# Attention: row maxima turned in squares of 32 by ScalarE and VectorE, not by TensorE, and a quarter of one block's sum moved from GpSimd to VectorE

## What is computed

```python
q = (x @ wq_w + wq_b).reshape(bs, sl, 32, 32)
k = (x @ wk_w + wk_b).reshape(bs, sl, 8, 32)
v = (x @ wv_w + wv_b).reshape(bs, sl, 8, 32)
attn = jnp.einsum('bqhfd,bkhd->bhfqk', qg, k) * scale     # qg: q with 4 heads for each key head
att = jax.nn.softmax(attn, axis=-1)
a = jnp.einsum('bhfqk,bkhd->bqhfd', att, v)
```

## Time and profile before

| | us |
|---|---|
| median of three timed runs | 2800.37 (2800.07 to 2800.58) |
| the profiled execution | 2795.91 |
| its span | 2794.1 |

### The profile page before, as it was taken

The page is one execution under the profiler, slowest core; times in us unless marked ns, Lnnn a source line. Parts: engine busy times, 40 slices in busy tenths (PEclk is TensorE's granted clock), DMA queues, the critical chain, the costliest instruction groups (busy, mean ns, idle before and its releaser), DMA issues.

```text
span 2794.1 us, 48987 instructions
## 1 busy us (share of the span) xinstructions
PE 2752.4 (99%) x14654; PEld 1695.8 (61%) x14654; DVE 2181.9 (78%) x2809; ACT 1529.4 (55%) x2959; POOL 1909.4 (68%) x710
## 2 busy tenths in 40 slices
PE   7999999999999999999999999999999999999998
PEld 4788888884444444444444444444444447888887
DVE  4433434348999999999999999999999968676667
ACT  3211111116777676777767777767777764455454
POOL 2433333317999999999999999999999996111110
PEclk9999999999999999999999999999999999999999
DMA  7544443434444334334334334344444443323332
GB/s 268 181 144 137 147 139 132 137 116 137 91 88 100 87 87 100 85 87 100 85 87 100 85 89 98 89 90 93 93 90 91 97 123 114 113 96 108 113 100 81
DMA packets 167645, 307.05 MB, mean 110 GB/s; under 512 B 50001, under 2 KB 91409, under 8 KB 159505
## 3 DMA queue, kind: packets, MB, share of 16 engines
q1 hardware_dynamic: 158496, 240.05, 29.5%
q0 software_dynamic: 9072, 66.06, 11.6%
HBM read 159.12 MB, written 79.82 MB: 86 GB/s over the span
## 4 chain that ended last, share of the span: by engine, by line
PE 74%; DVE 2%; ACT 0%; issue 0%; DVEq 0%; POOL 0%; ACTq 0%; POOLq 0%
PE back_ps L1348 22%; PE back_ps L1362 18%; PE s_ps L1322 17%; PE s_ps L1938 11%; PE back_ps L1379 2%; PE back_ps L1987 2%; PE back_ps L2006 1%; PE back_ps L1959 1%; DVE mx L1237 1%; PE back_ps L1337 0%; PE s_ps L1411 0%; DVE a_lo L1281 0%; ACT h_t L1719 0%; DVE two_sum L1252 0%; DVE xn L1793 0%
## 5 line engine op out<-in xcount | busy, mean ns | idle before, releaser
L1218 ACT ACTIVATE p_t<-back_ps 128x512 f32<-128x512 f32 x2048 | 1114.7, 596 | 432.5 <-PE back_ps L1348 390.7
L1237 DVE TENSOR_REDUCE mx<-s_ps 128x1 f32<-128x1024 f32 x1002 | 1172.4, 1208 | 83.9 <-PE s_ps L1322 76.2
L1128 POOL TENSOR_TENSOR p_sum<-p_sum,p_t 128x2048 f32<-128x2048 f32 x254 | 1166.2, 4591 | 24.8 <-ACT p_t L1218 7.9
L1348 PE MATMUL back_ps<-q_st,k_st 98*128 98x512 f32 x2048 | 809.9, 436 | 3.4 <-POOL ones L1097 2.4
L1348 PEld LDWEIGHTS back_ps<-q_st,k_st 98*128 98x128 f32 x2048 | 343.9, 187 | 592.1 <-ACT p_t L1218 495.7
L1322 PE MATMUL s_ps<-k_st,q_st 96*128 96x512 f32 x2004 | 633.0, 397 | 0.6 <-DVE mx L1237 0.3
L1362 PE MATMUL back_ps<-p_t,v_sb 128*32 128x512 f32 x4096 | 545.8, 605 | 0.0
L1322 PEld LDWEIGHTS s_ps<-k_st,q_st 96*128 96x128 f32 x2004 | 379.0, 189 | 72.5 <-DVE mx L1237 3.2
L574 POOL TENSOR_TENSOR o_lo<-side,o_hi 128x512 fp32r<-128x512 f32 x80 | 104.2, 1303 | 321.4 <-ACT o_hi L544 321.2
L1252 DVE TENSOR_REDUCE two_sum<-p_t 128x512 f32<-128x1024 f32 x256 | 317.8, 1243 | 2.1 <-ACT p_t L1218 2.1
L1128 POOL TENSOR_TENSOR p_sum<-p_t 128x2048 f32<-128x2048 f32 x64 | 312.9, 4889 | 8.6 <-ACT p_t L1218 8.6
(11 more groups left out here) (186 smaller groups left out, 2910.8 us busy)
## 6 DMA issues: line engine op xcount, KB each, us to landing
p_sum<-two_sum POOLq DMA_DIRECT2D x63, 1024.0 KB, 6.9
q_st<-q_hi_d SPq DMA_DIRECT2D x128, 256.0 KB, 4.3
stage<-w_mod SPq DMA_DIRECT2D x48, 512.0 KB, 6.4
q_hi_d<-o_hi SPq DMA_DIRECT2D x64, 256.0 KB, 2.0
q_lo_d<-o_lo SPq DMA_DIRECT2D x64, 256.0 KB, 2.0
q_st<-q_lo_d SPq DMA_DIRECT2D x64, 256.0 KB, 4.1
att_d<-a_sb SPq DMA_DIRECT2D x128, 128.0 KB, 2.3
a_f<-att_d SPq DMA_DIRECT2D x32, 512.0 KB, 4.6
```

The costliest lines, as they stand in the source:

```text
L1128: nc.gpsimd.tensor_tensor(total, before, p_t[:, kt, :, :], ALU.add).then_inc(sum_done, 1)
L1218: nc.scalar.activation(p_t[:, s, c, :], st_ps[:, c % 2, :], ACT.Exp, scale=SCALE)\
L1237: nc.vector.tensor_reduce(mx[:, slot % 2, e:e + 1], s_ps[:, e % 2, :], AX_X, ALU.max)\
L1348: nc.tensor.matmul(st_ps[:, c % 2, :], k_st[:, slot // 2, s * P:(s + 1) * P], q_st[:, slot, jj, h * QW:(h + 1) * QW], start=True, stop=True)\
```

## The change

The turn of the maxima leaves TensorE. ScalarE waits for the 16 maxima of a pair and rounds `mx` (128x16) to its high part, into the first 16 columns of a 128x32 tile `m_parts`, then writes the negated high part back beside the maxima. VectorE adds the two (a reduce of 16 pairs, so the low part) into the other 16 columns, waits for that, and turns the 128x32 tile in four squares of 32 into `m_rows`. A square holds 16 rows of high and 16 of low parts of 32 queries, so SP stores them by four DMAs of 32 rows of 128 bytes each, where there were two. The rows of `k_st` hold -1 instead of 1. The tiles are doubled by pair. The waits that shared the corner of `den_ps` with the turn go or are replaced.

Apart from this, in all pairs but the last, GpSimd adds only the columns 0 to 2 of block 2 (three quarters), and VectorE's fourth sum adds blocks 2, 3 and 4 of column 3 instead of 3 and 4. ScalarE's write of block 2 of the next pair therefore waits for VectorE's sums too.

```diff
+def put_rows(sp, q_st, slot, m_rows, landed):
+    rows = q_st[96:98, slot, :, :].bitcast(F32).rearrange("h j (t b r) -> h b (j t) r", b=4, r=32)
+    for b in range(4):
+        sp.dma_start(rows[:, b, :, :], m_rows[32 * b:32 * b + 32, slot % 2, :]).then_inc(landed, 16)
...
-    TURN_STEP = 5
+    MAX_STEP = 5
+    SHARED = 2
+    POOL_COLS = 3
...
         def put_max(pair, slot):
-            sp.wait_ge(m_lo_done, pair + 1)
-            for n, part in enumerate((m_hi, m_lo)):
-                sp.dma_start(q_st[STACK + n:STACK + n + 1, slot, :, :].bitcast(F32)
-                             .rearrange("o j s -> o (j s)"), part[:, :].bitcast(F32))\
-                  .then_inc(m_in, 16)
+            sp.wait_ge(m_turned, pair + 1)
+            put_rows(sp, q_st, slot, m_rows, m_in)
...
-                nc.gpsimd.tensor_tensor(total, before, p_t[:, kt, :, :], ALU.add).then_inc(sum_done, 1)
+                cols = slice(0, POOL_COLS if kt == SHARED and shares(pair) else REP)
+                nc.gpsimd.tensor_tensor(total[:, cols, :], before[:, cols, :], p_t[:, kt, cols, :], ALU.add)\
+                  .then_inc(sum_done, 1)
...
-        def max_hi(pair):
-            act.wait_ge(m_turned, pair + 1)
-            if not is_int(pair, 0):
-                act.wait_ge(m_in, pair * 32)
-            nc.scalar.activation(m_hi[:, :], m_ps, ACT.Copy, scale=-1.0).then_inc(m_hi_done, 1)
+        def max_hi(pair, slot):
+            act.wait_ge(max_done, pair * NS + NS)
+            if not below(pair, 2):
+                act.wait_ge(m_turned, pair - 1)
+            nc.scalar.copy(m_parts[:, slot % 2, 0:NS], mx[:, slot % 2, 0, :]).then_inc(m_hi_done, 1)
+            act.wait_ge(m_hi_done, pair + 1)
+            nc.scalar.activation(mx[:, slot % 2, 1, :], m_parts[:, slot % 2, 0:NS].bitcast(F32), ACT.Copy, scale=-1.0)\
+              .then_inc(m_back_done, 1)
...
-                    if c == 1 and s == TURN_STEP and not is_int(pair, NPAIR - 1):
-                        max_hi(pair + 1)
+                    if c == 1 and s == MAX_STEP and not is_int(pair, NPAIR - 1):
+                        max_hi(pair + 1, 1 - par)
...
-        def max_lo(pair):
-            dve.wait_ge(m_hi_done, pair + 1)
-            if not is_int(pair, 0):
-                dve.wait_ge(m_in, pair * 32)
-            nc.vector.scalar_tensor_tensor(m_lo[:, :], m_ps, -1.0, m_hi[:, :].bitcast(F32), ALU.mult,
-                                           ALU.subtract).then_inc(m_lo_done, 1)
+        def max_lo(pair, slot):
+            dve.wait_ge(m_back_done, pair + 1)
+            nc.vector.tensor_reduce(m_parts[:, slot % 2, NS:2 * NS].bitcast(F32),
+                                    mx[:, slot % 2, :, :].rearrange("p s e -> p e s"), AX_X, ALU.add)\
+              .then_inc(m_lo_done, 1)
+        def turn_max(pair, slot):
+            dve.wait_ge(m_lo_done, pair + 1)
+            if not below(pair, 2):
+                dve.wait_ge(m_in, pair * 64 - 64)
+            nc.vector.transpose(m_rows[:, slot % 2, :], m_parts[:, slot % 2, :].bitcast(F32)).then_inc(m_turned, 1)
...
-            nc.vector.tensor_reduce(two_sum[:, c, :], p_t[:, TWO:TWO + 2, c, :].rearrange("p s q -> p q s"),
+            first = SHARED if c >= POOL_COLS and shares(pair) else TWO
+            nc.vector.tensor_reduce(two_sum[:, c, :], p_t[:, first:TWO + 2, c, :].rearrange("p s q -> p q s"),
...
-                if s == TURN_STEP + 1 and not is_int(pair, NPAIR - 1):
-                    max_lo(pair + 1)
+                if s == MAX_STEP + 1 and not is_int(pair, NPAIR - 1):
+                    max_lo(pair + 1, slot + 1)
+                    turn_max(pair + 1, slot + 1)
...
-        def turn_max(pair, slot):
-            pe.wait_ge(max_done, pair * NS + NS)
-            if is_int(pair, 1):
-                pe.wait_ge(m_lo_done, 1)
-            elif not below(pair, 3):
-                pe.wait_ge(den_taken, pair - 2)
-            nc.tensor.matmul(m_ps, mx[:, slot % 2, :], ident[:, :], start=True, stop=True)\
-              .then_inc(m_turned, 1)
...
-                pe.wait_ge(m_in, pair * 32 + 32)
+                pe.wait_ge(m_in, pair * 64 + 64)
...
                 if s == SUM_STEP and not below(pair, 1):
-                    add_sum(pair - 1, (slot - 1) % 2)
-                if s == TURN_STEP and not is_int(pair, NPAIR - 1):
                     piece = piece_at(pair, slot % 2, it)
                     if piece:
                         pe.wait_ge(wo_lo_done, piece[1])
-                    turn_max(pair + 1, (slot + 1) % QR)
+                    add_sum(pair - 1, (slot - 1) % 2)
```

More of the change, by code:

```diff
@@ L124, in adaln_block @@
         m_at = k_at + 2 * S * 4 + 4 * 512 * 4
-        m_hi = keep("m_hi", [16, P], F32R)
-        m_lo = keep("m_lo", [16, P], F32R)
+        m_parts = keep("m_parts", [P, 2, 32], F32R)
+        m_rows = keep("m_rows", [P, 2, 32], F32)
+        mx = keep("mx", [P, 2, 2, 16], F32)
+        keep("m_rest", [P, 2 * P - 192], F32)
         assert nc.sbuf_base == m_at + 2 * P * 4
-        mx = keep("mx", [P, 2, 16], F32)
         s_ps = whole.enter_context(nc.psum_tensor("s_ps", [P, 2, S], F32))
-        ahead = Ahead(q_st, k_st, mx, m_hi, m_lo, s_ps, [sem(f"q_in{u}") for u in range(4)],
-                      [sem(f"k_in{u}") for u in range(2)], sem("s_ready"), sem("max_done"), sem("m_turned"),
-                      sem("m_hi_done"), sem("m_lo_done"), sem("m_in"),
+        ahead = Ahead(q_st, k_st, mx, m_parts, m_rows, s_ps, [sem(f"q_in{u}") for u in range(4)],
+                      [sem(f"k_in{u}") for u in range(2)], sem("s_ready"), sem("max_done"),
+                      sem("m_hi_done"), sem("m_back_done"), sem("m_lo_done"), sem("m_turned"), sem("m_in"),
                       [sem(f"qk_out{s}") for s in range(2)], [sem(f"v_out{s}") for s in range(2)])
@@ L473, in do @@
                         elif ev[0] == "negate":
-                            sp.wait_ge(ahead.m_lo_done, 1)
-                            for n, part in enumerate((ahead.m_hi, ahead.m_lo)):
-                                sp.dma_start(ahead.q_st[3 * HD + n:3 * HD + n + 1, 0, :, :].bitcast(F32)
-                                             .rearrange("o j s -> o (j s)"), part[:, :].bitcast(F32))\
-                                  .then_inc(ahead.m_in, 16)
+                            sp.wait_ge(ahead.m_turned, 1)
+                            put_rows(sp, ahead.q_st, 0, ahead.m_rows, ahead.m_in)
                         elif ev[0] == "rows":
@@ L781, in do @@
                             last.then_inc(ahead.s_ready, 1)
-                        elif ev[0] == "negate":
-                            pe.wait_ge(ahead.max_done, AHEAD - 3)
-                            nc.tensor.matmul(ahead.s_ps[0:16, 0, 0:P], ahead.mx[:, 0, :], ident[:, :],
-                                             start=True, stop=True).then_inc(ahead.m_turned, 1)
                         elif ev[0] == "group" and is_int(i, 0) and ev[1] < OBANKS:
@@ L895, in piece_at, with shares @@
         return two, (1 if is_int(pair, 1) else two + 2)
+    def shares(pair):
+        return not is_int(pair, NPAIR - 1)
     def below(i, value):
@@ L914, in sem @@
         return ctx.enter_context(nc.semaphore(name))
-    q_st, k_st, mx, m_hi, m_lo, s_ps = ahead.q_st, ahead.k_st, ahead.mx, ahead.m_hi, ahead.m_lo, ahead.s_ps
+    q_st, k_st, mx, s_ps = ahead.q_st, ahead.k_st, ahead.mx, ahead.s_ps
+    m_parts, m_rows = ahead.m_parts, ahead.m_rows
     p_t = sb("p_t", [P, NKT, REP, QW], F32)
@@ L1164, in await_bank @@
         def await_bank(pair):
-            if below(pair, 2):
-                act.wait_ge(m_lo_done, pair + 1)
-            else:
+            if not below(pair, 2):
                 act.wait_ge(den_taken, pair - 1)
@@ L1373, in add_sum @@
                 pe.wait_ge(joined, pair * 16 + 16)
-                if is_int(pair, NPAIR - 2):
-                    pe.wait_ge(den_taken, NPAIR - 2)
-                else:
-                    pe.wait_ge(m_lo_done, pair + 3)
+                if not below(pair, 1):
+                    pe.wait_ge(den_taken, pair)
             for c in range(REP):
```

43 lines of the change are left out of this document (23 added, 20 removed).

## The result

The changed kernel takes 2840.49 us (median of four runs, 2836.57 to 2844.15) against 2800.22 before: a ratio of 1.0145, interval 1.0132 to 1.0157. It is slower by 40 us. The profiled execution took 2844.15 us, with a span of 2842.3.

What follows compares the result with a forecast made beforehand. TensorE bounds the kernel at 26.04 us a pair, VectorE's loop close behind at 25.88. Adding 0.54 and 0.22 makes VectorE the bound at 26.64: +37.2 us altogether, 2837.5 us, range 2812 to 2880.

Steps and rivals of the forecast that it cites:

- VectorE's row from step 4 to the second maximum of step 0: Gapless VectorE work from step 4 of a pair's steps 0 to 7 into the next pair's step 0; 16.27 us.
- 0.16 us of slack: Claimed room per pair in the kernel before: VectorE's loop 25.88 us against TensorE's 26.04.
- The loop: VectorE's gapless row 16.27, hand-over to TensorE 1.18, two TensorE steps 6.20, wait for the next product 2.23: 25.88 us.
- Part (1): Turn of the maxima leaves TensorE: its own loop gets 0.20 us shorter, 25.84 a pair.
- Part (2): GpSimd's sum of block 2 loses a quarter, 1.16 us less a pair; worth 0 beyond the 0.23 it had free.
- Part (3): VectorE's fourth sum, in step 0, takes three blocks instead of two: +0.54 us a pair, 0.50 to 0.62.
- Part (4): VectorE's low part in step 6 becomes a small reduce and a dependent turn: +0.22 us, ends 0 and +0.65.
- Part (5): ScalarE's one operation of 0.27 us becomes two, some 0.5 us within 0.82 us of idle time: cost 0.
- Part (6): SP issues four row DMAs a pair instead of two, 0.3 us of slack: cost 0 unless landing exceeds 2.8 us.
- The sum: VectorE's loop becomes 26.64 us, +0.60 a pair over 61 pairs; +37.2 us altogether, giving 2837.5 us.
- The signs named beforehand: Later profile: loads wait on maxima some 0.8 us a pair, VectorE idles in steps 2 to 4, fourth sum 1.79 us.

Runs made afterwards that it cites:

- run 2: Kernel before with only the shared quarter: GpSimd leaves a quarter of block 2 to VectorE's fourth sum, TensorE still turns the maxima; 2830.68 us, ratio 1.0107.
- experiment 7: Changed kernel without the shared quarter, plus an unused VectorE reduce of 512 inputs: at step 3 2797.79 us, at step 0 2833.86 us.
- run 1: Changed kernel without the shared quarter: GpSimd adds all of block 2, VectorE's fourth sum takes two blocks; 2798.70 us, ratio 0.9995.
- run 4: Changed kernel, output not whole: a quarter of block 2 and the maxima's low part left out, reciprocal replaced by a two-column reduce; 2778.62 us, ratio 0.9924.
- run 6: Changed kernel with POOL_COLS 2: GpSimd adds two quarters of block 2, VectorE's third and fourth sums take three blocks each; 2879.16 us, ratio 1.0289.
- run 5: Changed kernel without the shared quarter, VectorE's fourth sum moved to step 1 and the division to steps 2, 2, 3; 2790.78 us, ratio 0.9966.
- experiment 8: Kernel of run 5 with GpSimd's join issued later, plus third sum and small operations moved (2821.54 us) or ScalarE's block-2 wait for sums dropped (2816.88 us).
- 10: Changed kernel whole, with the shared quarter, but VectorE's three-block fourth sum at step 1 and the division at steps 2, 2, 3; 2806.89 us, ratio 1.0033.

## Why the prediction was right

**Direction and size.** 2837.5 forecast, 2840.5 measured. The mechanism is shown: VectorE's row from step 4 to the second maximum of step 0 became the bound (period 26.64 forecast, 26.77 measured), run 2 fits the 0.16 us of slack that it had before, and the two runs of experiment 7 show that only work in this row counts.

**The loop.** The 25.88 us were worked out from the kernel before, in which VectorE did not bind. Five runs rest on it. With the added operations by their starts in VectorE's timelines (0.26 for the low part and turn, 0.67 for a third block, 0.59 for the reduce of experiment 7) it gives 26.55 in run 2 (measured 26.54), 26.14 in run 1 (26.15), 26.81 in the changed kernel (26.77), 27.48 with a second block (27.42) and 26.73 with the reduce in the tight row (26.70).

**Part (1)**, TensorE's loop at 25.84: 25.82 in run 4.

**Part (2)**, GpSimd's relief is worth nothing beyond 0.23: right. In the changed kernel and in run 6 it gained nothing; in run 5, where GpSimd does bind, it could be worth at most 25.99 - 25.82 = 0.17 a pair. The 0.23 itself was too large: that run's period puts GpSimd's whole round at 25.99, so it had 0.05 us free before, and after part (1) it would have been the next bound at 25.99 and not at 25.8.

**Part (3)** was mis-sized: 0.54 forecast, 0.62 to 0.66 measured by the periods and 0.67 by the starts. The step that was off is the rate of 1.064 ns an input; the third block costs some 1.27 ns an input (0.65 / 512). Experiment 7 has 0.56 for 512 inputs of another reduce, so the count alone doesn't give it. The prediction's upper end of 0.62 is the lowest of these, so it left no margin, and for its lower end of 0.50 it gives no working: its two rows give 0.54.

**Part (4)**: 0.22 forecast; by the starts 1407.32 to 1407.77 = 0.45, less the 0.19 of the old low part, 0.26. The first of the two takes 0.32 from start to start, the wait for its result among it, and the turn 0.13. Run 4, which leaves the first of them out, puts it at 0.33 or more with its wait. The rate of the Trainium skill, "VectorE: DVE Perf Modes", section "The TRN2 errata", gave an estimate of 0.19 for both. The trace does not agree: the two took 0.18 and 0.21 us, and 0.45 with the wait between them.

**Part (5)**, ScalarE's two operations cost nothing: right at step 5. The prediction's condition, that the last maximum ends before step 4 begins, is true of VectorE's step 4 alone. In the kernel before, VectorE's last two maxima of step 3 and TensorE's start of step 4 were

```profile
1401.49 2.36 DVE L1237 TENSOR_REDUCE mx<-s_ps 128x1 f32<-128x1024 f32 x2
```

```profile
1402.35 1.06 PE L1362 MATMUL back_ps<-p_t,v_sb 128*32 128x512 f32 x8
```

so the last maximum ended at 1403.85, 1.50 us after TensorE had begun the step. That did no harm at step 5 and failed in experiment 8, one step earlier: 0.97 us of waiting.

**Part (6)**, the rows: SP took 2.72 us to issue the four DMAs, 0.68 each (forecast 0.58), and TensorE's loads waited for them 14.7 us in 56 times, 0.26 each, where the prediction had 0.3 us to spare. In the changed kernel this lies in the stretch in which VectorE sets the pace anyway, and its period is no longer than the loop gives. Run 4 reaches 25.82 with the same DMAs, though its rows leave 0.3 us earlier. Cost 0, as forecast.

**The sum** had +37.2 us. The pairs gave (26.77 - 26.04) x 62 = 45 us, 8 more than forecast; the last stage gave 4 to 6 back (by 30 tiles of 0.22 us it is 6; all its tiles together took 443.4 us before and 439.5 in run 1), which no step of the prediction had. So the time is closer than the working deserved, and that part is luck: two errors of opposite sign. The profiled execution of the changed kernel shows a third thing, two tiles of the last stage that took 17.57 and 16.15 us one behind the other, where runs 1, 5 and 10 have 16.5 to 17.4 and 12.5 to 12.8 in that place; it lies 3.7 us above its median. The cause is open.

**The signs named beforehand.** Waits of the loads on maxima in every pair: there, twice the 0.8 us named (104.3 / 62 = 1.7), most of it hidden by the matmuls still running. Idle time of VectorE in the light steps: 0.43 and 0.42. GpSimd waits for ScalarE once a pair: there, 132.1 us in 65 times, 2.0 each. The fourth sum at 1.79 us: no, 1.92.

## What to carry to other kernels

An engine's busy share doesn't say how near it is to being the bound: VectorE had 1.24 us a pair free and only 0.16 before it held TensorE up. Add up the loop through the engine's tight row (its row without a gap, the hand-over, the steps until it starts again), and put a new operation into a step in which the engine idles; the same reduce cost 36 us in one step and none three steps on.

Before moving a wait, list who stands behind each of its two ends. Hiding GpSimd's 0.66 us moved the landing of its DMA into VectorE's tight row, and starting ScalarE's operations a step early put them ahead of their input; both kernels had been expected to gain some 10 us and lost over 20, against the kernel of 5 that they started from. That these waits are the reason is read from the traces; no run isolates it.
